# Pair sums and weight sums of the first down projection: accumulating DMAs and VectorE in place of GpSimd

## What is computed

```python
def cond(x, ...):                      # 4 x 64 there; here x is 8 x 128 x 512, f32
    gate = lora_add(x @ W_gate.T, x, A_gate, B_gate)     # F = 1376, rank 16, adapter per batch entry
    up   = lora_add(x @ W_up.T,   x, A_up,   B_up)
    act  = silu(gate) * up
    return lora_add(act @ W_down.T, act, A_down, B_down)
def ffn(x, ...):                       # I = 1792
    nx = x * rsqrt(mean(x * x) + 1e-5) * ln_w
    return (silu(nx @ gate_w.T) * (nx @ up_w.T)) @ down_w.T
out = x + ffn(cond(x))
```

## Time and profile before

| | us |
|---|---|
| median of 3 runs | 413.83 (413.66 to 415.65) |
| the profiled execution, its time | 414.94 |
| its span in the trace | 412.9 |
| PE busy | 393.1 (95%) |
| VectorE / ScalarE / GpSimd busy | 346.1 / 252.3 / 47.0 |
| bytes moved by DMA | 38.96 MB |

### The profile page before, as it was taken

How to read it: one execution, slowest core, us unless ns; L and a number is a source line. 1 busy time by engine, 2 the same in 40 slices (tenths; PEclk the granted TensorE clock), 3 DMA queues, 4 the chain that set the end, 5 groups by cost and what they waited for, 6 DMA issues and landing times.

```text
span 412.9 us, 5738 instructions
## 1 busy us (share of the span) xinstructions
PE 393.1 (95%) x1954; PEld 324.7 (79%) x1954; DVE 346.1 (84%) x475; ACT 252.3 (61%) x390; POOL 47.0 (11%) x34
## 2 busy tenths in 40 slices
PE   9999999999996993699989999999999999999997
PEld 5999888888874782588858788888888888888886
DVE  4799987777588889989999988787787869899994
ACT  5879786767666387387365554655556567375730
POOL 6300000000155149213000000000000000000000
PEclk9999999999998898699989999999999999999999
DMA  7530263111587593400020113131212123205112
GB/s 261 176 124 6 75 171 104 51 50 44 198 182 193 181 228 64 112 4 0 0 104 0 52 52 102 51 103 51 103 52 102 48 93 120 121 2 193 51 51 102
DMA packets 15517, 38.96 MB, mean 94 GB/s; under 512 B 2434, under 2 KB 4994, under 8 KB 15490
## 3 DMA queue, kind: packets, MB, share of 16 engines
q1 hardware_dynamic: 13360, 32.19, 23.0%
q0 software_dynamic: 1008, 4.59, 6.3%
q10 hardware_dynamic: 1122, 1.84, 1.3%
HBM read 36.51 MB, written 2.10 MB: 94 GB/s over the span
## 4 chain that ended last, share of the span: by engine, by line
PE 83%; DVE 10%; issue 4%; ACT 3%; DVEq 0%; ACTq 0%
PE bank L1605 48%; PE bank L1968 16%; PE bank L1860 5%; PE bank L1823 3%; PE bank L1777 3%; DVE xs L1074 3%; PE bank L1812 3%; PE bank L1615 2%; DVE ws L1074 2%; ACT xs L540 1%; PE bank L1718 1%; PE bank L1771 1%; DVE last_wd L1074 1%; DVE down_w L1074 1%; DVE wsum L1086 1%
## 5 line engine op out<-in xcount | busy, mean ns | idle before, releaser
L1605 PE MATMUL bank<-xs,ws 128*128 128x512 f32 x840 | 198.7, 394 | 2.7 <-DVE mu L1133 1.7
L1605 PEld LDWEIGHTS bank<-xs,ws 128*128 128x128 f32 x840 | 158.0, 190 | 37.2 <-DVE mu L1133 2.4
L540 ACT ACTIVATE xs<-act 128x512 fp32r<-128x512 f32 (+1 forms) x73 | 50.1, 703 | 38.5 <-PE bank L1860 10.4
L1074 DVE TENSOR_TENSOR xs<-act,xs 128x512 fp32r<-128x512 f32 (+1 forms) x66 | 54.2, 839 | 3.0 <-ACT xs L540 2.4
L1074 DVE TENSOR_TENSOR ws<-wraw,ws 128x256 fp32r<-128x256 f32 (+2 forms) x45 | 32.2, 718 | 14.4 <-ACT ws L540 14.3
L540 ACT ACTIVATE bank<-bank 128x512 f32<-128x512 f32 x34 | 19.4, 578 | 38.4 <-PE bank L1605 33.2
L1074 DVE TENSOR_TENSOR ws<-wsum,ws 128x1024 fp32r<-128x1024 f32 x20 | 28.2, 1409 | 16.6 <-ACT ws L540 16.6
L1860 PE MATMUL bank<-xs,down_w_sums 128*128 128x512 f32 x120 | 30.4, 410 | 9.5 <-DVE xs L1074 9.5
L540 ACT ACTIVATE mu<-bank 128x512 f32<-128x512 f32 x44 | 26.1, 596 | 21.7 <-PE bank L1605 16.1
L1968 PE MATMUL bank<-xs,vs 128*128 128x512 f32 x168 | 38.2, 389 | 0.0
L1968 PEld LDWEIGHTS bank<-xs,vs 128*128 128x128 f32 x168 | 31.5, 188 | 6.5
(11 more groups left out here) (146 smaller groups left out, 509.7 us busy)
## 6 DMA issues: line engine op xcount, KB each, us to landing
wraw<-wgu_in SPq DMA_DIRECT2D x22, 512.0 KB, 3.3
down_w_sums_raw<-wc_in POOLq DMA_DIRECT2D x7, 640.0 KB, 8.5
wdr<-vs_in SPq DMA_DIRECT2D x7, 512.0 KB, 3.3
wraw<-vj_in SPq DMA_DIRECT2D x3, 896.0 KB, 4.7
down_w_sums_raw<-wc_in SPq DMA_DIRECT2D x4, 640.0 KB, 5.0
down_w_raw<-wc_in SPq DMA_DIRECT2D x3, 640.0 KB, 4.3
xa<-xT_in SPq DMA_DIRECT2D x4, 256.0 KB, 4.2
xa<-xT_in ACTq DMA_DIRECT2D x2, 512.0 KB, 5.2
```

Of the source, the lines that this page charges most:

```text
L540: return nc.scalar.activation(out_ap, in_ap, ACT.Copy, scale=scale)
L1074: return nc.vector.tensor_tensor(out_ap, raw, v32(part), ALU.subtract)
L1605: ins = mm(z[:, :], w_slot(j)[:, w, s, k * P:(k + 1) * P], xs[:, c, r, k, :], start=(start and k == 0 and s == 0 and r == 0), stop=(k == 1 ...
```

## The change

The t1 differences move to VectorE (`t1`, three instructions, each ahead of the matching part of CT4's lo), and all other sums that GpSimd computed become accumulating DMAs that it issues: t3, t2 and t4 in seven DMAs within `act` (768, 256, 512, 512, 512, 512 and 256 KB; those of t2 and t4 take two tiles each), with counters for even and odd ones. The sums of groups G1+1, G1+2 and G1+3 (the first two were VectorE's) are made by a plain load of a base (512 KB, SP), an accumulating load `two_w` (384 KB) and an accumulating DMA within `wsum`, `more_w` (256 KB). w10 is loaded before CT4, and C22 before CT1. Several steps move on ScalarE and VectorE: `hi_b`/`lo_b` of group G1 from group 7 to behind CT2's parts; `keep_u2` ahead; the second half of w10 from between CT3's parts to behind CT4's; and others below. PE does the last `p4` of the first stage after item 1, not 0. `square_hi` is moved ahead of the copy of x's block 21. The GpSimd DMA scratch is doubled to 2048. In the weight sums done by VectorE, sums 2 and 3 are made in the other order.

```diff
-W11, W12, W22, WS3, WS1, WS2, WS4 = range(7)
+W11, W12, W22, WS3, WS1, WS4, WS2 = range(7)
...
-        CW_ORDER = (C11, CT2, CT3, C21, CT4, CT1, C22)
+        CW_ORDER = (C11, CT2, CT3, C21, CT4, C22, CT1)
...
+            def load_base(j):
+                sp.wait_ge(s_wblo, j - 2)
+                sp.dma_start(wsum[:, :, :], wbase_in[j - G1 - 1].rearrange("p (a m) -> p a m", a=4)).then_inc(s_wbase, 16)
+
+            load_base(G1 + 1)
             load_w(G1 + 2)
+            load_base(G1 + 2)
             load_w(G1 + 3)
+            load_base(G1 + 3)
...
-            def pair_sum(to, more, op=ALU.add):
-                nc.gpsimd.tensor_tensor(to, to, more, op).then_inc(s_tp, 1)
...
+            def add_act(n, to, more):
+                if n >= 2:
+                    pool.wait_ge(*t_added(n - 2))
+                nc.gpsimd.dma_start(to, more, accum_op=ALU.add).then_inc(s_t_add[n % 2], 16)
+
+            def two_w(j):
+                n = j - G1 - 1
+                pool.wait_ge(s_wbase, 16 * n + 16)
+                nc.gpsimd.dma_start(wsum[:, 0:3, :], wmore_in[n].rearrange("p (a m) -> p a m", a=3), accum_op=ALU.add
+                                    ).then_inc(s_wadd, 16)
+
+            def more_w(j):
+                pool.wait_ge(s_wadd, 32 * (j - G1 - 1) + 16)
+                nc.gpsimd.dma_start(wsum[:, 2:4, :], wsum[:, 1:2, :].to_broadcast([P, 2, 256]), accum_op=ALU.add
+                                    ).then_inc(s_wadd, 16)
...
+            pool.wait_ge(s_clo, KC * C11 + 4)
+            pool.wait_ge(*t_added(T3_012))
+            add_act(T2_23, act_c(2, 4, 0), act_c(2, 4, 1))
+            pool.wait_ge(*cw_loaded(C22))
+            add_w(S4_21, C22, 1, 0)
+            two_w(G1 + 1)
+            pool.wait_ge(s_clo, KC * C21 + 2)
+            add_act(T4_01, act_c(KC, KC + 2, 0), act_c(0, 2, 0))
+            pool.wait_ge(*cw_loaded(CT1))
+            add_w(S1_21, CT1, 1, 0)
+            more_w(G1 + 1)
+            pool.wait_ge(s_clo, KC * C21 + 4)
+            add_act(T4_23, act_c(KC + 2, KC + 4, 0), act_c(2, 4, 0))
             add_w(S4_22, C22, 1, 1)
+            pool.wait_ge(s_clo, KC * C21 + 5)
             pool.wait_ge(s_last, 2)
+            add_act(T4_4, act_c(KC + 4, KC + 5, 0), act_c(4, 5, 0))
...
+            def t1(n):
+                k, end = C_PARTS[CT1][n]
+                v.wait_ge(s_clo, KC * CT2 + end)
+                for half in range(k // 2, (end - 1) // 2 + 1):
+                    v.wait_ge(*t_added(T4_01 + half))
+                part = act_c(k, end, 0)
+                nc.vector.tensor_tensor(part, part, act_c(KC + k, KC + end, 1), ALU.subtract).then_inc(s_t1, 1)
...
-                if k == 0:
+                if k == 1:
                     p4(S1 - 1)
...
-            hi_a(G1 + 3)
             square(6)
             sum_hi(1)
+            square_hi()
             a.wait_ge(s_nx, 4)
             hi_x(1, X21, nx0[:, 2:4, :])
-            square_hi()
-            hi_b(G1 + 3)
+            hi_a(G1 + 3)
```

More of the change, by code:

```diff
@@ L203, in cw_added, with t_added @@
             return s_cw_add[n % 2], 16 * (n // 2 + 1)
-        S2_21, S3_21, S2_22, S1_21, S4_21, S4_22, S4_11 = range(7)
-        T3_012, T3_3, T2_0, T2_12, T2_3, T4_01, T4_23, T4_4, T1_0, T1_12, T1_34 = range(1, 12)
+        def t_added(n):
+            return s_t_add[n % 2], 16 * (n // 2 + 1)
+        S2_21, S3_21, S2_22, S4_21, S1_21, S4_22, S4_11 = range(7)
+        T3_012, T3_3, T2_01, T2_23, T4_01, T4_23, T4_4 = range(7)
         SEED, KEEP_U2, COPY_U3, COPY_P5 = 0, 2, 4, 6
@@ L397, in _ @@
             load_down_w(C21, 0, 1)
-            sp.wait_ge(s_p3, S1)
-            load_down_w(CT4, 1, 1)
-            sp.wait_ge(s_p4, S1)
-            load_down_w(CT1, 1, 1)
-            load_down_w(C22, 0, 1)
             sp.wait_ge(s_c22f, S1 // 2)
@@ L534, in _ @@
-            pool.wait_ge(s_wsum, 3 * g + 2)
-            nc.gpsimd.tensor_tensor(wsum[:, 3, :], wsum[:, 2, :], raw_w[:, 2, :], ALU.add).then_inc(s_wsum, 1)
+            for j in range(G1 + 2, G1 + 4):
+                two_w(j)
+                more_w(j)
         @block.scalar
@@ L959, in _ @@
             hi_w(CT3, cw_added(S3_21))
-            hi_c(CT2, 0)
             hi_w(CT2, cw_added(S2_22))
-            hi_c(CT2, 1)
-            hi_c(CT2, 2)
+            for n in range(3):
+                hi_c(CT2, n)
+            hi_b(G1)
             hi_w(C21, cw_loaded(C21))
@@ L995, in _ @@
                 square(m)
-            hi_c(CT1, 1)
-            hi_b(G1 + 2)
+            hi_a(G1 + 2)
             keep_y(2)
@@ L1005, in _ @@
             sum_hi(0)
-            hi_w(C22, cw_added(S4_11))
             hi_c(C22, 1)
             hi_c(C22, 2)
+            hi_b(G1 + 2)
             rsqrt(0)
@@ L1455, in _ @@
             lo_w(CT3)
-            lo_c(CT2, 0)
             c21(S1 - 1)
             lo_w(CT2)
-            lo_c(CT2, 1)
-            lo_c(CT2, 2)
+            for n in range(3):
+                lo_c(CT2, n)
+            lo_b(G1)
             lo_w(C21)
@@ L1463, in _ @@
             lo_c(CT2, 3)
-            lo_c(C21, 0)
-            sums(G1 + 1)
-            lo_c(C21, 1)
-            lo_c(C21, 2)
+            for n in range(3):
+                lo_c(C21, n)
             lo_w10(0)
             lo_short(0)
-            lo_w(CT4)
-            lo_a(G1 + 1)
             lo_c(CT3, 0)
             lo_c(CT3, 1)
+            lo_a(G1 + 1)
+            lo_c(CT3, 2)
+            lo_w(CT4)
+            lo_b(G1 + 1)
+            for n in range(3):
+                t1(n)
+                lo_c(CT4, n)
             lo_w10(1)
-            lo_c(CT3, 2)
-            lo_b(G1 + 1)
-            sums(G1 + 2)
+            lo_c(CT1, 0)
             lo_w(CT1)
-            for n in range(3):
-                lo_c(CT4, n)
-            lo_c(CT1, 0)
+            lo_c(CT1, 1)
             v.wait_ge(s_lnw, 16)
             nc.vector.tensor_scalar(lnw[:, :], lnw[:, :], 0.375 / (H * H), 0.0, ALU.mult, ALU.add).then_inc(s_lnws, 1)
+            add_square(0, 1)
             lo_a(G1 + 2)
-            add_square(0, 1)
-            lo_c(CT1, 1)
-            lo_b(G1 + 2)
             add_square(0, 2)
             lo_c(CT1, 2)
+            lo_w(C22)
             lo_c(C22, 0)
@@ L1493, in _ @@
             sum_lo(0)
-            lo_w(C22)
             lo_c(C22, 1)
             lo_c(C22, 2)
+            lo_b(G1 + 2)
             norm(0)
```

120 lines of the change are left out of this document (56 added, 64 removed).

## The result

| | before | after |
|---|---|---|
| median (range), 20 executions each | 414.84 (413.45 to 416.25) | 417.30 (413.41 to 420.47) |
| ratio, 95% interval | | 1.0047 [1.0026, 1.0068] |
| the profiled execution, its span | 414.94, 412.9 | 418.55, 416.7 |
| bytes moved by DMA | 38.96 MB | 45.90 MB |

The change makes the kernel some 0.5% slower, at the edge of what can be told; the forecast was +1.4% (419.7). Medians and ranges here are of all executions, while the ratios leave out an execution that took over 1.5% more than the fastest of its kernel (one of after, two of `again`, three of `w10_early`, one of `pair_dmas_only`).

What follows compares the result with a forecast made beforehand. PE was busy 95% of the span, so only its gaps and low-clock stretches could be won. Terms +5.2 (later resume at `short_c`), +1.7 (clock), -1.0 (last wait) gave +5.9: 413.83 to 419.7 us; range 408 to 431.

Steps and rivals of the forecast that it cites:

- early gaps: PE's two gaps before `t_c` ends: both close with VectorE free, 6.3 us of gaps and low clock, `t_c` through at 138.6.
- rate of the additions: Accumulating DMAs in GpSimd's queue were taken to move 172 KB per us, against 358 for plain loads.
- the first place: CT2, waiting for T2_23 (landing at 145.9): starts at 150.1, 5.2 us later than before, after a gap of 11.5 us.
- Rival 1: Sums within SBUF run at the plain rate, 358 KB/us: -4.9 us, 408.9; chance 0.17 (below 411.8).
- Rival 2: Each 2 KB packet has a fixed price: +7.9 us, 427.6 at 125 KB/us; chance 0.20 (above 424).
- Rival 3: The DMAs are never last and all gaps close: 395 us; chance 0.05.
- what moves beside the queue: Plain loads sharing the engines with the additions: 4096 KB, 11.4 us, before CT2; 3 x 512 KB, 4.3 us, before `short_c`.
- The second place: `short_c`, waiting for w10's second half behind T4_4 (179.4): PE resumes at 182.3, 5.2 us later, after a 9.6 us gap.
- The clock: PE's low clock behind the gap at `short_c`: costs 1.7 us again.
- The tail: From `short_c` to the next stage: same PE work; `square_hi` moved ahead may win 1.0 of the last wait's 1.7 us.
- The base of the sum: The sum of +5.9 us was added to the median 413.83 of the kernel before, giving 419.7.

Runs made afterwards that it cites:

- again: The changed kernel run once more without an edit, on the chip of its variants: 416.69 us, ratio 1.001 to the kernel before.
- w10_early: Changed kernel with the second half of w10 back between CT3's parts on ScalarE and VectorE: 415.09 us, ratio 0.9963 to the kernel before.
- pair_dmas_only: Changed kernel with the three groups' weight sums on VectorE and no base loaded, pair sums still DMAs: 415.65 us, ratio 0.9996 to the kernel before.
- thin_pairs: Changed kernel with each pair-sum DMA adding only the first 64 of 512 columns: 406.41 us, ratio 0.9799 to the kernel before.
- t4_first: Changed kernel with t4's DMAs ahead of G1+1's weight sums and S1_21, that group's hi/lo behind CT4's parts and w10: 411.86 us, ratio 0.9899 to before.
- hold_loads: Changed kernel with SyncE waiting for T2_23 before it loads CT4, C22 and CT1: 415.56 us, ratio 1.0015 to the kernel before.
- square_back: Changed kernel with square_hi back behind the copy of X21 and hi_a(G1+3) ahead of square(6): 417.70 us, ratio 1.0101 to the kernel before.
- before_dve: The kernel before with all 14 of GpSimd's sums issued by VectorE, no DMA added: 407.01 us, ratio 0.9811 to the kernel before.
- dve_pair_sums: Changed kernel with the seven pair-sum DMAs (t3, t2, t4) done on VectorE, weight sums still DMAs: 404.42 us, ratio 0.9772 to the kernel before.
- dve_pairs_both: `dve_pair_sums` with w10's second half between CT3's parts and G1+1's weight-sum hi/lo behind CT4's parts: 401.70 us, ratio 0.9674 to the kernel before.
- late_b2: `dve_pairs_both` with the hi of G1+2's weight sums behind copy_p5 and its lo behind y_1(1): 398.55 us, ratio 0.9603 to the kernel before.

## Why the prediction was wrong, by its own steps

| step | forecast | measured |
|---|---|---|
| early gaps close, `t_c` ends | 138.6 | 137.8 |
| rate of the additions, KB/us | 172 | 180 and 171 |
| T2_23 landed | 145.9 | 144.2 |
| CT2 starts | 150.1 | 148.5 |
| CT3 ends | 172.7 | 170.7 |
| base issued, landed | 149.6, 154.7 | 148.4, 155.9 |
| T4_4 landed | 179.4 | 177.2 |
| PE resumes at `short_c` | 182.3 | 180.3 |
| clock behind that gap | +1.7 | +2.7 |
| last wait ahead of the next stage | -1.0 | -1.1 |
| clock behind that wait | 0 | -1.1 |
| span, after less before | +5.9 | +3.8 |

The measured column is the one profiled execution of after; its times at the first place are uncertain by 1 to 2 us (`again` and the traces with the same code).

**The mechanism was right at both places:** the early gaps close, ScalarE waits for T2_23, then for the base's sums and T4_4, PE has two gaps of 10.7 and 9.6 us (11.5 and 9.6 forecast) and a low clock behind each, q0 moves 9.96 MB in 13.5%. `thin_pairs`, `t4_first` and `pair_dmas_only` each take one of these causes away, and the gap it was to make goes or shrinks.

**Rival 1** (SBUF-to-SBUF sums at the plain rate) fell: at 358 KB per us for its 1536 KB of such sums the second stretch would have had q0 busy for 14 us, and it was for 18.9. The Trainium skill's 436 GB/s for SBUF to SBUF ("SBUF — State Buffer", Summary: rules for kernel authors) is no rate for sums: here q0 moves 9.96 MB in 0.135 x 416.7 = 56.3 us of all 16 engines, 177 GB/s. **Rival 2** (a fixed price for each packet) fell as well: what the change adds to q0 is 3024 packets and 5.37 MB, 563 packets per MB where before had 220, and it took 56.3 - 26.0 = 30.3 us, again 177 GB/s. **Rival 3** fell: the DMAs are last twice.

**The terms that were mis-sized** are, first, those of what moves beside the queue. PE resumed at `short_c` 3.2 us later than before where +5.2 was forecast, the clock behind it cost 1.0 us more than its term, and 1.1 us behind the last wait were not in the sum. The second place is the clearer one: the forecast had PE resume at 182.3, and it does at 179.3 to 180.3 in all three traces with that code. There I counted 1536 KB of plain loads, 4.3 us; q1 moved 1.02 MB in 0.119 x 21 = 2.5 us, since the base of G1+2 is issued only at 170. That is 1.8 of the 2.2 us by which T4_4 came earlier. The base took 7.5 us and not 5.1, because CT1's 640 KB and S4_21's addition were still moving beside it; issued 1.2 us earlier, it was there 1.2 us later. The windows of 4 to 5 us from 160 to 174 have a share of 1.05 to 1.13, so the two kinds overlap by more than an addition of times allows, and that makes this good. At the first place the queue was quicker than I took it (22.0 for 23.1 us) and the share was 1.03 over 34 us, 1.0 us of overlap; the plain bytes were fewer, 3.65 MB (3564 KB) for 4096 KB, but each was dearer beside the queue (11.9 us for 11.4). Together T2_23 came 1.7 us earlier; over the seven traces with this code it came 0.2 to 3.7 us earlier than forecast. `hold_loads` doesn't size the tail of the plain loads, since its 1.5 us lie within that spread.

**The clock** behind the second gap cost 2.7 us (2.93 for 1.60 and 4.95 for 3.59), where I took 1.7 from one row. (That row was itself read 0.2 too small: CT3's 8.71 us were compared with CT2's 6.97, where 30 matmuls without a wait ahead start 6.80 us before the next.) `again` has 2.8 us there and `square_back` 1.3, so one row could not give this term to better than a microsecond. **The tail** had the right size by luck: I forecast 1.0 us for the move of `square_hi`, and `square_back` gives 0.35 us to it. And the 1.1 us behind it, where before has a granted clock of 0.68 at 210 to 215 and after 1.00, I had not forecast.

**The base of the sum.** Terms of the span give +3.8, the profiled executions +3.6, but the medians of 20 only +2.5: the one profiled execution of after lies 1.25 above its median, that of before 0.1 above its own. And the median of 3 that I added the sum to was 1.0 under that of 20. So of the miss of 3.4 us in the difference (5.9 forecast, 2.5 measured), 2.1 are terms of the sum, 0.2 lies outside the span, 1.1 is the one execution that was profiled. The direction came out, though only just; a clear loss (1.4% forecast, 0.5% measured) did not, since errors of 1 to 2 us in five terms leave of +5.9 us less than I took as sure.

**Where the gain went.** `before_dve` shows what taking the sums from GpSimd is worth alone: 7 to 8 us. The change takes it, and gives back 10: 3328 KB of sums went to the queue that was already at a share of one, to spare VectorE 8 us that it had free. That is the part that the change should not have had (`dve_pair_sums`, some 12 us faster than after). The weight sums as DMAs did no harm once nobody that PE waits for stood behind their wait (`pair_dmas_only` and `dve_pairs_both` against `late_b2`).

**Still open:** why a gap of the same length costs 1.3 us of clock in one trace and 2.7 in another, even at the same place of the same code, and why after's executions spread more than before's. The five kernels in which the queue isn't last at CT2 spread over 1.3 to 3.0 us (4 or 5 executions each), the others with the change's DMAs over 4.5 to 9.8 (4 to 20 each); that the queue's timing is the source is argued, not shown. The eight traces under `hold_loads`, in which T2_23 lands up to 3.5 us apart, fit it.
